# Cross attention: four of seven row units turned in 32x32 blocks on VectorE and through DRAM, instead of on TensorE

## The chip, the cores and the metric

The kernel runs on one core of one Trainium2 chip. The metric is the device time of one execution in microseconds (us). Five engines work side by side: TensorE (PE), VectorE (DVE), ScalarE (ACT), GpSimd (POOL) and SyncE (SP), which here only issues transfers. Sixteen DMA engines move the data.

## The reference

One decoder layer: self attention, cross attention and a mixture of experts, each followed by a residual and a norm. Both kernels differ only in the middle part and in what its memory layout drags along. Cut to that part (32 batches of 56 rows, 1500 context positions, 16 heads of width 128 on 8 key heads):

```
q = (x @ Wq) split in 16 heads          # x: (32, 56, 256)
k, v = ctx @ Wk, ctx @ Wv               # ctx: (32, 1500, 128)
attn = softmax(q @ k.T / sqrt(128) + mask)
x = layernorm(x + (attn @ v) merged @ Wo)
```

The kernel folds Wk into the query side and Wv with Wo into one matrix M per head, so scores are q' @ ctx.T and the output is (attn @ ctx) @ M. Every fp32 product is made of three products of rounded parts, hi*hi + hi*lo + lo*hi.

## The kernel before

It has three phases: phase_a (folded weights, self attention, queries), phase_b (cross attention) and phase_c (routing and experts). Phase_b is about three quarters of the time, and the change is there.

A batch has 16 * 56 = 896 query rows, which are 7 units of 128 rows. A slot is 4 units (even) or 3 units (odd); a pair of batches has 4 slots. Each slot takes CH = 12 steps, so a batch has 24 steps. All engines run the same list of steps in program order, each step with a few pieces of work of different age:

- fill (L817 to L819): three matmuls write 128 rows x 500 scores to one of 3 score banks. VectorE adds the mask, takes the maximum and writes the scores to SBUF (scores, L983), then makes the shift (L991). ScalarE takes the exponential of a unit of 1500 (L901).
- turn (L831): 15 steps later TensorE turns one chunk of 125 positions of every unit of the slot, 128x125 to 125x128, to a turn bank in PSUM. ScalarE rounds it to pT_hi (L895), VectorE makes the rest pT_lo (L997).
- weigh (L850 to L852): two steps later TensorE multiplies the context chunk by pT_hi and pT_lo and sums over the 12 chunks in an output bank.
- the reciprocals of the softmax sums (L1004) are stored to DRAM as single words, 4 bytes each, 512 words for an even slot and 384 for an odd one (store_rden, L908), and fetched again as a row for all partitions (load_rden, L917). VectorE scales the output by them (L1025). After each pair TensorE projects (L860).

SyncE issues the transfers in one order written by hand: q_in, cT_in, mask_in and c_in for each batch (L750 to L766), each after GpSimd has split the one before it in hi and lo (L1099, L1101), and the store of the result (L774). ScalarE's queue issues L908 and L917.

Of the kernel before, what the change touches and what calls it, by code (L numbers as in the profile page):

```python
# [26 lines left out]
ALU = mybir.AluOpType  # L27
# [22 lines left out]
CK = CTX // CH  # L50
FILLS = 3
FW = CTX // FILLS
ROWS = XH * S
UNITS = (4, 3)
SLOTS = 4
WIDE = UNITS[0] * 128
# [11 lines left out]
for width in (NT, EXPERTS * EXPERTS, 128, RP, RP, NT, NT * EXPERTS, 128):  # L68
# [8 lines left out]
Attention = namedtuple("Attention", "sync tensor scalar vector gpsimd edge tail q_split cT_split c_split fill_done fill_taken "  # L77
                       "first_batch_weighed weighed third_slot_turned all_lo projected z_taken y2_stored")
# [45 lines left out]
def phase_a(nc, D, semaphore, M_hi, M_lo, q_in, cT_in, ident, ident_loaded):  # L124
    with ExitStack() as ctx:
# [107 lines left out]
        def sync(sp, load_ahead):  # L233
# [56 lines left out]
            def store_last():  # L290
                store_q(NBLK - 1, range(PARTS))
# [4 lines left out]
            return store_last  # L296
# [331 lines left out]
def phase_b(nc, D, semaphore, edge, opening, M_hi, M_lo, q_in, cT_in, ident, const_loaded):  # L628
    with ExitStack() as ctx:
        def sb(name, shape, dt=F32):  # L630
            edge[name] = nc.sbuf_base
            return ctx.enter_context(nc.sbuf_tensor("b_" + name, shape, dt))

# [9 lines left out]

        oT = sb("oT", [128, XH, 2, S])
        oT_hi = sb("oT_hi", [128, XH, 2, S], F32R)
        oT_lo = sb("oT_lo", [128, XH, 2, S], F32R)
        y1_res = sb("y1_res", [PAIR, F])
# [4 lines left out]
        sb("spare", [128, 2480])  # L652
        pT_hi = sb("pT_hi", [CK, 3, WIDE], F32R)
        pT_lo = sb("pT_lo", [CK, 3, WIDE], F32R)
        p = [None, sb("p1", [128, UNITS[1], CTX])]
        rden_all = sb("rden_all", [128, 2, WIDE])
# [6 lines left out]
        c_in = sb("c_in", [CK, CH * CD])  # L663
        c_hi = sb("c_hi", [CK, 2, CH * CD], F32R)
        c_lo = sb("c_lo", [CK, 2, CH * CD], F32R)
        mask_in = sb("mask_in", [128, CTX], U8)
        mask_add = sb("mask_add", [128, 2, CTX], BF16)
        half = sb("half", [PAIR, 1])
        top = sb("top", [128, 2, UNITS[0], FILLS + 1])
        top_min = sb("top_min", [128, FILLS + 1])  # L670
        shift = sb("shift", [128, 2, UNITS[0]])
        den = sb("den", [128, 2, UNITS[0]])
        rden = sb("rden", [128, 2, UNITS[0]])
        p[0] = sb("p0", [128, UNITS[0], CTX])
        edge["end"] = nc.sbuf_base
# [3 lines left out]
        q_loaded, cT_loaded, c_loaded, mask_loaded = sem("q_loaded"), sem("cT_loaded"), sem("c_loaded"), sem("mask_loaded")  # L679
        res_loaded, y2_stored = sem("res_loaded"), sem("y2_stored")  # L680
        q_split, cT_split, c_split, mask_ready = sem("q_split"), sem("cT_split"), sem("c_split"), sem("mask_ready")
# [3 lines left out]
        rden_done, rden_stored = sem("rden_done"), sem("rden_stored")  # L685
        rden_loaded = [sem("rden_loaded_even"), sem("rden_loaded_odd")]
# [4 lines left out]
        STEPS = SLOTS * CH  # L691
        TURN_LAG = CH + 3
        PV_LAG = TURN_LAG + 2


        RDEN_AT, STORE_AT, LOAD_AT = 3, 4, 11
        SCALE_AT, ROUND_AT = 4, 5
        LATE_SLOTS, LOAD_LATE, SCALE_LATE = range(2), 2, 3
        PROJECT_AT, NORM_AT, NORM_OUT_AT = CH + 10, CH + 11, 2 * CH + 8
        OT_OPS = 2  # L700
        TAIL = PV_LAG + 3
# [7 lines left out]
        def units(slot):  # L709
            return UNITS[slot % 2]  # L710

        unit0 = [sum(units(k) for k in range(slot)) for slot in range(SLOTS + 1)]
        PUNITS = unit0[SLOTS]
        PFILLS = FILLS * PUNITS

        def fills_at(n):

            slot, k = n // CH, n % CH
            count = FILLS * units(slot)
            return [(slot, m) for m in range(count) if m * CH // count == k]  # L720

        def slot_before(i, slot, k):

            return i + (slot - k) // SLOTS, (slot - k) % SLOTS

# [1439 lines left out]
```

## Time and profile before

| | |
|---|---|
| time, median of 3 runs | 1717.78 us (1717.73 to 1717.91) |
| span of the profiled execution | 1718.6 us |
| mean granted TensorE clock | 0.994 |
| TensorE busy | 1685.0 us, 98% |
| VectorE busy | 1221.3 us, 71% |
| ScalarE busy | 937.2 us, 55% |
| GpSimd busy | 664.6 us, 39% |
| moved by DMA | 140.29 MB, mean 82 GB/s |

The profiled execution has no time of its own beside its span; the span is 0.8 us above the median of the runs. A line such as "L983 DVE ... x672 | 451.9, 673 | 58.9" says that line 983 of the kernel ran 672 times on VectorE, was busy for 451.9 us in all, took 673 ns each and that its engine idled 58.9 us just before it.

### The profile page before, as it was taken

Reading aid. Unit: us, or ns where it says so; the run is one execution under the profiler, and the core shown is the slowest. Engines: PE = TensorE matmul, PEld = TensorE weight load, DVE = VectorE, ACT = ScalarE, POOL = GpSimd, SP = SyncE. Lnnn points to the kernel's source line nnn. Section 1 sums busy time; section 2 is a strip of 40 time slices with the busy share of each in tenths; the row PEclk is TensorE's granted clock in tenths of the full one; section 3 lists DMA queues with packets and bytes.
Section 4 is the critical chain, followed back from the end, with each engine's and each line's share of the span. In section 5 each row is a group of like instructions: output and inputs, shape, how many; then the busy total and the mean of one; then the engine's idle time right before and its main releaser. Section 6 shows DMA issues by size and latency. Waiting matters only on the chain.

```text
span 1718.6 us, 28903 instructions
## 1 busy us (share of the span) xinstructions
PE 1685.0 (98%) x10034; PEld 1517.0 (88%) x10034; DVE 1221.3 (71%) x3377; ACT 937.2 (55%) x1717; POOL 664.6 (39%) x417
## 2 busy tenths in 40 slices
PE   7999999999999999999999999999999999999996
PEld 7998889898989898989898989989898989888985
DVE  5655676877787878777778777776878787756557
ACT  5444465656565656565656565565656565644543
POOL 1220344525243333333334343443525341355435
PEclk9999999999999999999999999999999999999998
DMA  5234643423141423333232323232324130431433
GB/s 197 81 132 130 193 95 78 70 68 81 54 97 41 90 44 88 48 86 68 62 68 63 68 63 68 70 66 77 74 61 89 52 57 12 112 114 40 121 90 95
DMA packets 102856, 140.29 MB, mean 82 GB/s; under 512 B 37022, under 2 KB 81728, under 8 KB 102592
## 3 DMA queue, kind: packets, MB, share of 16 engines
q1 hardware_dynamic: 60784, 115.47, 26.8%
q10 hardware_dynamic: 38912, 14.80, 4.0%
q0 software_dynamic: 3024, 8.26, 1.8%
q8 instruction: 79, 1.29, 0.4%
q14 instruction: 57, 0.47, 0.2%
HBM read 113.62 MB, written 24.89 MB: 81 GB/s over the span
## 4 chain that ended last, share of the span: by engine, by line
PE 93%; DVE 2%; issue 1%; ACT 1%; DMA 1%; POOL 0%; another core or an unknown queue 0%; POOLq 0%; SPq 0%; ACTq 0%; DVEq 0%
PE b_turn L831 17%; PE b_out L850 9%; PE b_out L851 9%; PE b_out L852 9%; PE b_score L817 9%; PE b_score L819 9%; PE b_score L818 9%; PE b_out L860 5%; PE a_bank L344 5%; PE c_gate L1513 2%; PE c_down L1540 1%; PE a_bank L370 1%; PE a_bank L395 1%; PE a_bank L424 1%; PE a_bank L417 1%
## 5 line engine op out<-in xcount | busy, mean ns | idle before, releaser
L895 ACT CAST b_pT_hi<-b_turn 125x512 fp32r<-125x512 f32 (+1 forms) x768 | 406.8, 530 | 543.0 <-PE b_turn L831 539.8
L997 DVE TENSOR_TENSOR b_pT_lo<-b_turn,b_pT_hi 125x512 fp32r<-125x512 f32 (+1 forms) x768 | 478.0, 623 | 259.7 <-ACT b_pT_hi L895 254.2
L983 DVE CUSTOM_DVE_ANT_0 b_p<-b_score,b_mask_add 128x500 f32<-128x500 f32 x672 | 451.9, 673 | 58.9 <-PE b_turn L831 24.4
L831 PEld LDWEIGHTS b_turn<-ident,b_p 128*125 128x125 f32 x2688 | 409.4, 186 | 55.2
L831 PE MATMUL b_turn<-ident,b_p 128*125 128x128 f32 x2688 | 418.1, 272 | 0.0
L901 ACT ACTIVATE b_p<-b_p,b_shift 128x1500 f32<-128x1500 f32 x224 | 347.5, 1551 | 2.1 <-DVE b_top_min L991 2.1
L850 PE MATMUL b_out<-b_pT_hi,b_c_hi 125*128 125x512 f32 (+1 forms) x768 | 346.5, 451 | 0.7 <-DVE b_pT_lo L997 0.6
L1135 POOL TENSOR_TENSOR b_oT_lo<-b_oT,b_oT_hi 128x896 fp32r<-128x896 f32 x32 | 67.6, 2112 | 624.5 <-ACT b_oT_hi L925 588.0
L851 PE MATMUL b_out<-b_pT_lo,b_c_hi 125*128 125x512 f32 (+1 forms) x768 | 280.9, 366 | 0.0
L852 PE MATMUL b_out<-b_pT_hi,b_c_lo 125*128 125x512 f32 (+1 forms) x768 | 280.5, 365 | 0.0
L817 PE MATMUL b_score<-b_cT_hi,b_q_hi 128*128 128x500 f32 x672 | 262.9, 391 | 0.0
L819 PE MATMUL b_score<-b_cT_hi,b_q_lo 128*128 128x500 f32 x672 | 260.2, 387 | 0.0
L818 PE MATMUL b_score<-b_cT_lo,b_q_hi 128*128 128x500 f32 x672 | 259.8, 387 | 0.0
L852 PEld LDWEIGHTS b_out<-b_pT_hi,b_c_lo 125*128 125x128 f32 x768 | 144.2, 188 | 17.9
L819 PEld LDWEIGHTS b_score<-b_cT_hi,b_q_lo 128*128 128x128 f32 x672 | 126.1, 188 | 25.8
L850 PEld LDWEIGHTS b_out<-b_pT_hi,b_c_hi 125*128 125x128 f32 x768 | 145.7, 190 | 1.5 <-DVE b_pT_lo L997 1.4
L851 PEld LDWEIGHTS b_out<-b_pT_lo,b_c_hi 125*128 125x128 f32 x768 | 145.9, 190 | 0.0
L818 PEld LDWEIGHTS b_score<-b_cT_lo,b_q_hi 128*128 128x128 f32 x672 | 128.1, 191 | 14.2
L817 PEld LDWEIGHTS b_score<-b_cT_hi,b_q_hi 128*128 128x128 f32 x672 | 126.2, 188 | 14.1
L1101 POOL TENSOR_TENSOR b_c_lo<-b_c_in,b_c_hi 125x1536 fp32r<-125x1536 f32 x32 | 111.9, 3497 | 2.7
L1101 POOL TENSOR_TENSOR b_cT_lo<-cT_in,b_cT_hi 128x1500 fp32r<-128x1500 f32 x31 | 106.3, 3428 | 2.6
L860 PE MATMUL b_out<-M_lo,b_oT_hi 128*112 128x256 f32 x256 | 71.8, 280 | 0.0
(250 smaller groups left out, 2402.1 us busy)
## 6 DMA issues: line engine op xcount, KB each, us to landing
cT_in<-in_ctxT SPq DMA_DIRECT2D x32, 750.0 KB, 9.8
b_c_in<-in_ctx SPq DMA_DIRECT2D x32, 750.0 KB
q_store<-a_fold_in_or_q_stage SPq DMA_DIRECT2D x16, 896.0 KB, 4.2
q_in<-q_store SPq DMA_DIRECT2D x32, 448.0 KB, 7.1
b_rden_all<-rden_store ACTq DMA_DIRECT2D x32, 256.0 KB, 3.6
b_rden_all<-rden_store ACTq DMA_DIRECT2D x32, 192.0 KB, 3.7
b_mask_in<-in_mask SPq DMA_DIRECT2D x32, 187.5 KB, 9.4
slot_store<-c_y2T SPq DMA_DIRECT2D x35, 128.0 KB, 1.7
```

The source lines that it names most:

```text
L817: pe.matmul(out, q_hi[b][:, rows], cT_hi[b][:, keys], start=True, stop=False)
L818: pe.matmul(out, q_hi[b][:, rows], cT_lo[b][:, keys], start=False, stop=False)
L819: pe.matmul(out, q_lo[b][:, rows], cT_hi[b][:, keys], start=False, stop=True).then_inc(fill_done, 1)
L831: mm = pe.transpose(turn_bank[n % 3][0:CK, u * 128:(u + 1) * 128], p[slot % 2][:, u, c * CK:(c + 1) * CK], ident[:])
L850: pe.matmul(out, hi, pT_hi[:, n % 3, 0:w], start=(c == 0), stop=False)
L851: pe.matmul(out, hi, pT_lo[:, n % 3, 0:w], start=False, stop=False)
L852: pe.matmul(out, lo, pT_hi[:, n % 3, 0:w], start=False, stop=(c == CH - 1)).then_inc(pv_done, 1)
L895: act.copy(pT_hi[:, n % 3, 0:w], turn_bank[n % 3][0:CK, 0:w]).then_inc(hi_done, 1)
L901: act.activation(row, row, ACT.Exp, bias=shift[:, slot % 2, u:u + 1], scale=float(X_SCALE), accum_out=den[:, slot % 2, u:u + 1]).then_inc( ...
L983: dve.tensor_tensor_reduce(out=p[slot % 2][:, u, keys], in0=score_bank[j][:, 0:FW], in1=mask_add[:, b, keys], scale=1.0, scalar=-3.0e38, o ...
L997: dve.tensor_tensor(pT_lo[:, n % 3, 0:w], turn_bank[n % 3][0:CK, 0:w], pT_hi[:, n % 3, 0:w].bitcast(F32), ALU.subtract).then_inc(lo_done, 1)
L1101: pool.tensor_tensor(lo, src, hi.bitcast(F32), ALU.subtract).then_inc(done, 1)
```

## The change

The four units of the even half of a batch are no longer turned by TensorE. Their way to the weighing is new:

1. VectorE turns each unit in 32x32 blocks with one instruction over 4 x 12 x 32 = 1536 elements (turn_blocks), at steps 5, 9, 13 and 17 of the batch, into one tile, by_block. It waits until the store of the block before it has landed.
2. SyncE stores by_block to DRAM, 128 partitions of 6144 bytes (store_p), one store for each unit.
3. After the next batch's first such store, SyncE issues 16 fetches (load_keyed): for each unit four, each filling 32 partitions with 4 rows of 1536 bytes. Together they fill keyed, 128 partitions of 16 x 384 words, one buffer.
4. ScalarE rounds each chunk to pT_hi (keyed_round), GpSimd makes the rest in place (keyed_rest) and TensorE weighs it (weigh_even) in steps 16 to 27 after the batch's own 24.

The three odd units still go by TensorE. The loop goes by batches of 24 steps instead of pairs. The roundings of the context parts move from GpSimd to ScalarE (cT_round at step 1, c_round at step 8). The stores of the reciprocals stand at step 16 (even) and at step 2 of the next batch (odd). The context values have two buffers, c_raw, loaded once the batch two before is weighed. The projection is spread over 4 steps. Phase_c gets a new memory layout and a longer tail of steps (24 to 52).

```diff
+            def store_p(m, u):
+                sp.wait_ge(blocks_turned, EVEN * m + u + 1)
+                if m >= 2:
+                    sp.wait_ge(keyed_loaded, 16 * QUADS * EVEN * (m - 1))
+                sp.dma_start(D["p"][m % 2, u].rearrange("q a n -> q (a n)"),
+                             by_block[:].rearrange("q al b j -> q (al b j)")).then_inc(p_stored, 16)
+            def load_keyed(m, u):
+                if m:
+                    sp.wait_ge(pv_done, whole(m - 1))
+                sp.wait_ge(p_stored, 16 * EVEN * (m + 1))
+                for a in range(QUADS):
+                    sp.dma_start(keyed[32 * a:32 * (a + 1), QUADS * u:QUADS * (u + 1), :],
+                                 D["p"][m % 2, u, :, a].rearrange("(b i) n -> i b n", i=32)).then_inc(keyed_loaded, 16)
...
+            for m in range(B):
+                if m >= 2:
+                    load_c(m)
+                if m:
+                    store_p(m, 0)
+                    for u in range(EVEN):
+                        load_keyed(m - 1, u)
+                if m + 2 < B:
+                    load_q(m + 2)
+                if m:
+                    store_p(m, 1)
+                store_p(m, 2)
+                if m + 2 < B:
+                    load_cT(m + 2)
+                    load_mask(m + 2)
+                store_p(m, 3)
...
+            def turn_blocks(m, u):
+                dve.wait_ge(exp_done, PUNITS * m + u + 1)
+                dve.wait_ge(p_stored, 16 * (EVEN * m + u))
+                own = row(m, u)
+                keys = bass.AP(own.tensor, own.offset, [own.ap[0], [32, QUADS], [CK, CH], [1, 32]])
+                dve.transpose(by_block[:], keys).then_inc(blocks_turned, 1)
...
+            def keyed_round(m, c):
+                if c == 0:
+                    act.wait_ge(keyed_loaded, 16 * QUADS * EVEN * (m + 1))
+                act.wait_ge(pv_done, STEPS * m + CH + c - 2)
+                act.copy(by_blocks(pT_hi[:, c % 3, :]), keyed_chunk(keyed, c)).then_inc(hi_done, 1)
...
+            def keyed_rest(m, c):
+                pool.wait_ge(hi_done, STEPS * m + CH + c + 1)
+                pool.tensor_tensor(keyed_chunk(keyed_lo, c), keyed_chunk(keyed, c),
+                                   by_blocks(pT_hi[:, c % 3, :]).bitcast(F32),
+                                   ALU.subtract).then_inc(keyed_lo_done, 1)
```

## Rows read from the trace of the kernel before

**Rows 1.** The page: busy time of the engines.
```profile
PE 1685.0 (98%) x10034; PEld 1517.0 (88%) x10034; DVE 1221.3 (71%) x3377; ACT 937.2 (55%) x1717; POOL 664.6 (39%) x417
```
**Rows 2.** The page: the chain of work that ended last.
```profile
PE 93%; DVE 2%; issue 1%; ACT 1%; DMA 1%; POOL 0%; another core or an unknown queue 0%; POOLq 0%; SPq 0%; ACTq 0%; DVEq 0%
PE b_turn L831 17%; PE b_out L850 9%; PE b_out L851 9%; PE b_out L852 9%; PE b_score L817 9%; PE b_score L819 9%; PE b_score L818 9%; PE b_out L860 5%; PE a_bank L344 5%; PE c_gate L1513 2%; PE c_down L1540 1%; PE a_bank L370 1%; PE a_bank L395 1%; PE a_bank L424 1%; PE a_bank L417 1%
```
**Rows 3.** The timeline, ScalarE's queue: DMA issues of the reciprocals (start, duration).
```profile
709.94 0.33 ACTq L917 DMA_DIRECT2D b_rden_all<-rden_store  x1
718.80 0.38 ACTq L908 DMA_DIRECT2D rden_store<-b_rden  x1
736.88 0.38 ACTq L908 DMA_DIRECT2D rden_store<-b_rden  x1
791.88 0.33 ACTq L917 DMA_DIRECT2D b_rden_all<-rden_store  x1
```
**Rows 4.** The timeline, TensorE in one step with four units.
```profile
739.02 0.39 PE L817 MATMUL b_score<-b_cT_hi,b_q_hi 128*128 128x500 f32 x1
739.71 0.60 PE L831 MATMUL b_turn<-ident,b_p 128*125 128x128 f32 x4
740.07 0.47 PE L850 MATMUL b_out<-b_pT_hi,b_c_hi 125*128 125x512 f32 x1
740.38 0.40 PE L851 MATMUL b_out<-b_pT_lo,b_c_hi 125*128 125x512 f32 x1
740.61 0.40 PE L852 MATMUL b_out<-b_pT_hi,b_c_lo 125*128 125x512 f32 x1
```
**Rows 5.** Groups by line and shape.
```profile
L983 DVE CUSTOM_DVE_ANT_0 b_p<-b_score,b_mask_add 128x500 f32<-128x500 f32 x672 | 451.9, 673 | 58.9 <-PE b_turn L831 24.4 <-PE b_score L819 14.9
L983 DVE DVE_READ_ACCUMULATOR2_ANT b_top<- 128x1 f32 x672 | 55.6, 83 | 0.0
L997 DVE TENSOR_TENSOR b_pT_lo<-b_turn,b_pT_hi 125x512 fp32r<-125x512 f32 x384 | 264.6, 689 | 187.2 <-ACT b_pT_hi L895 183.0 <-issue 0.5
L997 DVE TENSOR_TENSOR b_pT_lo<-b_turn,b_pT_hi 125x384 fp32r<-125x384 f32 x384 | 213.4, 556 | 72.6 <-ACT b_pT_hi L895 71.1 <-issue 0.5
L895 ACT CAST b_pT_hi<-b_turn 125x512 fp32r<-125x512 f32 x384 | 224.1, 584 | 311.1 <-PE b_turn L831 309.3 <-issue 1.8
L1101 POOL TENSOR_TENSOR b_cT_lo<-cT_in,b_cT_hi 128x1500 fp32r<-128x1500 f32 x31 | 106.3, 3428 | 2.6
```
**Rows 6.** Windows: engines' busy time, granted clock, DMA share, GB/s; fastest stretch.
```profile
16.00:20.00 4.00, 4.00 (x32) 3.35 (x31) 2.08 (x4) 1.00 (x4) 0.00 (x0) 1.00 1.06 441
```
**Rows 7.** The timeline, SyncE's queue: a fetch of c_in, and two fetches of cT_in.
```profile
703.53 0.29 SPq L766 DMA_DIRECT2D b_c_in<-in_ctx  x1
721.31 0.33 SPq L756 DMA_DIRECT2D cT_in<-in_ctxT  x1
755.46 0.35 SPq L756 DMA_DIRECT2D cT_in<-in_ctxT  x1
```
**Rows 8.** Windows behind these issues.
```profile
706.00:709.00 3.00, 3.00 (x28) 3.00 (x27) 0.00 (x0) 0.00 (x0) 0.00 (x0) 1.00 0.31 131
722.00:724.00 2.00, 2.00 (x14) 1.89 (x13) 1.80 (x6) 1.96 (x4) 0.67 (x1) 1.00 2.33 48
...
726.00:728.00 2.00, 2.00 (x15) 1.86 (x14) 1.87 (x6) 1.37 (x2) 0.00 (x0) 1.00 0.57 24
...
730.00:732.00 2.00, 2.00 (x13) 1.81 (x12) 1.78 (x8) 0.95 (x3) 0.00 (x0) 1.00 0.97 324
757.00:760.00 3.00, 3.00 (x19) 2.67 (x17) 2.61 (x10) 1.12 (x4) 0.00 (x0) 1.00 0.89 299
```
**Rows 9.** All landings of cT_in, of 750 KB each.
```profile
DMA to landing us min/median/max: 4.3/9.8/11.3
```
**Rows 10.** The page, DMA issues (count, KB each, median us to landing).
```profile
q_store<-a_fold_in_or_q_stage SPq DMA_DIRECT2D x16, 896.0 KB, 4.2
slot_store<-c_y2T SPq DMA_DIRECT2D x35, 128.0 KB, 1.7
```

More of the change, by code:

```diff
@@ new lines, in fills_at, with unit_ends, parity, behind @@
+        def fills_at(n):
+            return [f for f in range(PFILLS) if fill_step(f) == n]
+        def unit_ends(n, late):
+            return [f // FILLS for f in range(FILLS - 1, PFILLS, FILLS) if fill_step(f) + late == n]
+        def parity(u):
+            return (0, u) if u < EVEN else (1, u - EVEN)
+        def behind(m, n, at, count=1):
+            for k in range(3):
+                if at <= n + STEPS * k < at + count and 0 <= m - k:
+                    return m - k, n + STEPS * k - at
+            return None
@@ new lines, in units_behind, with row, whole, keyed_chunk @@
+        def units_behind(m, n, late, last):
+            ends = [] if last else [(m, u) for u in unit_ends(n, late)]
+            return ends + ([(m - 1, u) for u in unit_ends(n + STEPS, late)] if m else [])
+        def row(m, u):
+            return p[0][:, (EVEN * m + u) % EVEN_DEEP, :] if u < EVEN else p[1][:, u - EVEN, :]
+        def whole(m):
+            return STEPS * (m + 1)
+        def keyed_chunk(tensor, c):
+            return tensor[0:CK, :, 32 * c:32 * (c + 1)]
+        def by_blocks(ap):
+            return ap.rearrange("p (g j) -> p g j", j=32)
@@ L797, in sync @@
-            loads(1, first=True)
-            with sp.Fori(2, NPAIR) as i:
-                loads(i)
-            store(NPAIR - 2)
-            residual(NPAIR - 1)
+                load_mask(0)
+                load_c(0)
+            store_last_part, wait_stored = opening.sync(sp, load_ahead)
+            load_q(1)
+            load_cT(1)
+            load_mask(1)
+            load_c(1)
+            for part in range(len(opening.stored)):
+                if part >= 2:
+                    store_p(0, part - 2)
+                store_last_part(part)
@@ L854, in project @@
-            def project(i):
-                pe.wait_ge(oT_lo_done, 2 * (i + 1))
-                for h in range(XH):
+                    if m == 0:
+                        pe.wait_ge(*opening.taken[1])
+                    else:
+                        pe.wait_ge(oT_done, OT_OPS * (2 * m - 1))
+                    pe.wait_ge(c_lo_done, m + 1)
+                pe.wait_ge(lo_done, CH * m + c + 1)
+                out, (hi, lo) = out_bank[1][:, 0:w], values(m, c)
+                pe.matmul(out, hi, pT_hi[:, c % 3, 0:w], start=(c == 0), stop=False)
@@ L861, in project @@
                                        start=(h == 0 and n == 0), stop=(h == XH - 1 and n == len(terms) - 1))
[L862 to L878 removed]
+                if part == parts - 1:
+                    mm.then_inc(proj_done, 1)
@@ L1224, in phase_c @@
         count_r = queries.take("c_count_r", [1, RP])
-        places_2, tiles_2 = odd.again(), odd.again()
+        ones, half = queries.take("c_ones", [128, 128]), queries.take("c_half", [128, 1])
+        turned_p.at = edge["p1"] - 2 * 4 * H_DEEP * 512
         h_hi = turned_p.take("c_h_hi", [128, H_DEEP, 512], F32R)
```

787 lines of the change are left out of this document (403 added, 384 removed).

## The prediction

> **What bounds the kernel now.** I read the page first: TensorE is busy for 98% of the span, VectorE for 71%, ScalarE 55%, GpSimd 39% [rows 1]. The chain of waits says the same of the path: 93% is TensorE, and the turning L831 alone is 17% of it [rows 2]. So matmuls in program order set the time. The fetch of the reciprocals that closes a pair of batches is issued at 709.94 and again at 791.88 [rows 3]: 81.94 us for two, 41.0 us a batch. Whatever is taken from TensorE is gained until something else takes longer than the rest of the batch. Transfers matter nowhere yet. So I next look for what the new transfers would cost.
>
> **What is removed.** One step of an even slot shows four turnings at 739.71 and the weighing behind them at 740.07, 0.36 us. The first weighing matmul takes 0.31 us to the next, the others 0.23 [rows 4], 0.08 more, which I also lay to the turnings. 12 steps x 0.44 = 5.3 us a batch. With nothing else in the way the batch would take 41.0 - 5.3 = 35.7 us.
>
> **What VectorE gets.** It loses 12 rests of 512 columns, 12 x 0.689 = 8.3 us, and gets four block turnings of 1536 elements. No row shows one. The two shapes of L997 differ by 133 ns for 128 columns [rows 5], 1.04 ns an element and 0.16 us fixed: 1.76 us each, 7.0 us in all. Bounds: half the time per element (0.96 us) and twice (3.4 us). With 21 scorings at 0.673 + 0.083, 12 odd rests at 0.556 [rows 5], and some 4 us of small work, VectorE has about 33.6 us in a batch: just below 35.7, no bound yet but no reserve either. After a stall it can't catch up.
>
> **What ScalarE and GpSimd get.** ScalarE rounds as often as before, 0.584 us [rows 5], from SBUF now, and two context parts more (some 3.3 us): it has 45% idle, which hides it. GpSimd gets 12 rests of 512 elements: 3428 ns for 1500 is 2.29 ns each [rows 5], so 1.2 us, 14 us a batch on an engine that had 16 us of work in 41. It fits, 1.2 us against 1.4 us for a TensorE step. Both cost nothing while their inputs are there.
>
> **What the transfers cost: the ring.** The step that I think decides is the order of SyncE's queue. Block turning 2 (step 13) overwrites the one block tile and waits for store 1. Store 1 stands in the queue behind store 0, all 16 fetches and the fetch of q. I follow the ring from the end of block turning 0, taking transfers as served in the order of issue:
> - issue 0.4; store 0, 0.786 MB at the fastest rate that the trace shows, 441 GB/s [rows 6], 1.8
> - the 16 fetches, 3.146 MB: K
> - q, 0.459 MB: 1.0; store 1: 1.8; landing 1.4 (128 KB take 1.7 to land [rows 10], less 0.3 of moving): together 6.4 + K
> - block turning 2, 1.76, and the scoring behind it, 0.76: 2.5. TensorE can be three banks ahead and no more, so it stands at the fill of step 18 until then.
> - TensorE from step 18 to the fill of step 5 of the next batch: 10 fills at 0.69 and 10 weighings of 512 columns at 0.70 [rows 4], an odd weighing of 0.5, three turnings of three units at 0.33, and the last fill 0.7: 16.1
> - VectorE scores, makes a rest and turns block 0: 0.76 + 0.56 + 1.76 = 3.1
>
> The sum is 28.1 + K a batch, if that is more than 35.7.
>
> **K.** No row shows a fetch that fills 32 partitions. Above it stands 441 GB/s, reached with all 128 partitions: 7.1 us. Below stands the only big fetch here that doesn't go over all 128, c_in with 125: issued at 703.53 [rows 7], it runs at 131 GB/s [rows 8]; at that rate K is 24.0 us. The new fetches resemble neither end more; I take the geometric middle, 240 GB/s and K = 13.1 us.
>
> The Trainium skill has a rule that speaks against this edit ("SBUF — State Buffer", the DMA port swizzle): a fetch to partitions 0 to 31 reaches only 8 of 16 ports, some 218 GB/s at best. With it K would be 14.4, the batch 1.3 longer, and the time below 40 us longer. No run so far shows it.
>
> **The fetch of c and the store of single words.** The fetch of c_in (0.768 MB at 131 GB/s, 5.9 us) now stands just before store 0. Counting from the landing of store 1, the weighing that frees its buffer ends at about 16.3 us and block turning 0 at 21.7: alone it adds at most 0.5. But the trace shows a hole. The even reciprocals, 512 words of 4 bytes, are stored at 718.80 [rows 3]; cT_in is issued at 721.31 [rows 7], and the DMA moves 48 and 24 GB/s in the windows at 722 and 726, and 324 only from 730 [rows 8]. The cT_in issued at 755.46 meets no store, and 299 GB/s flow at 757 [rows 7, 8]. Landings of cT_in between 4.3 and 11.3 us say it for all 32 [rows 9]. So behind such a store everything stands for some 11 us. In the new order the odd store (384 words) is issued at about 14.2 us of the same count, right ahead of the c fetch. Behind the odd store of before (736.88, [rows 3]) nothing was issued for ten microseconds, so its hole isn't seen: nothing, or by words three quarters of 11.2, 8.4 us. Then c starts at 22.6 and ends at 28.5, and store 0 is 6.4 us late. Bounds for this term c: 0.5 to 6.4; I take 3. The even store's hole (step 16) falls on cT_in, mask and store 3, which have 11 steps until they are waited for; I cost it at nothing, and if that cover is gone block turning 0 is late next.
>
> The skill's page "DMA: Bandwidth & Descriptors" (Specifications) says that below 512 B the engines read, modify and write. The hole above agrees in kind; by that rule the odd store would have its hole too, c would be 6.4 and the time some 105 us above my forecast.
>
> **Sum.** 28.1 + 13.1 + 3.0 = 44.2 us a batch, 3.2 above 41.0. Over 31 batches +99 us. Once: the last batch's fetches have no fills to hide under. They start at step 27, take K + 2 = 15 us, and some 9 us of odd turning and weighing cover them: +6. The first batch runs at VectorE's pace, some 25 us against about 19 us of matmuls: +6. Against the span, 1718.6 + 111 = 1830; against the median of the runs, 0.8 lower, **1829 us**.
>
> **Rivals.**
> - *The transfers keep up (ends faster).* The fetches run near 441 GB/s and the odd store makes no hole. The ring is 28.1 + 7.1 + 0.5 = 35.7, TensorE's own sum. 1717.8 - 31 x 5.3 + 12 = 1566 us. It decides from K + c below 12.9: with c = 0.5 fetches faster than 254 GB/s. For it: a store of q in small rows, 896 KB, lands in 4.2 us [rows 10]. Against it: c_in's 131 and the hole. All of its cases up to no change together: 24%.
> - *The transfers are worse than I take.* K above 18 or the whole hole: with K = 18 and c = 6.4 the batch takes 52.5, 1717.8 + 31 x 11.5 + 12 = 2086; with K = 24 it is 58.5 and 2272. For it: c_in's row; that even and odd store make two holes in a batch. Against: c_in's row has a shape that no new fetch has. 17%.
> - *VectorE is the bound.* The transfers keep up, but a block turning takes 3.4 us: 33.6 + 6.4 = 40.0 a batch, 1717.8 - 31 x 1.0 + 12 = 1699. For it: no row of that operation. Against: every VectorE row runs near 1 ns an element. 5%.
> - *My forecast*, the ring between 42 and 50 us: 54%.
>
> **Range and chances.** The forecast alone gives 1760 to 2010. The first rival has its bulk at 1566 to 1640, and I can't leave all of it out: 1590 to 2000. A change of 0.2% (3.4 us) is what a measurement can tell here. Faster 27% (the first rival without its last sliver, and most of the third), same 3%, slower 70%.
>
> **What would show it.** In the profile after: the period of a batch from two issues of the same line; TensorE's busy share clearly below 98% with idle time before the fills or the even weighing, released by VectorE's scoring or GpSimd; VectorE's block turning waiting on the DMA of store_p, at the third of the four most; a ScalarE wait at its first keyed round on keyed's DMA. The rate in the windows where only the 16 fetches move gives K at once: 441, 240 or 131 GB/s. A window near 0 GB/s behind the odd store shows c; if bytes flow there, that term falls. If block turning 2 doesn't wait, the ring is wrong, and either TensorE runs at 35.7 us a batch or a cause I haven't named sets it. If the stores pass the fetches in the engines, my assumed order of service falls, and with it most of the loss.

## The result and the profile after

The changed kernel takes **2190.88 us** (median of 4 runs, 2184.44 to 2195.93), the kernel before 1717.76 beside it: ratio 1.2751, 95% interval 1.2723 to 1.2778. It is slower, as forecast, but by 473 us, not by 111, and outside the range. The profiled execution has a span of 2192.8 us and a mean granted clock of 0.894 (0.994 before).

The page of the kernel after (these answer to [rows 1, 2]; then, in 40 equal slices of the span, TensorE's busy tenths, the granted clock in tenths and the DMA share in tenths):

```profile
PE 1684.7 (77%) x8498; PEld 1437.7 (66%) x8498; DVE 1189.4 (54%) x3134; ACT 1018.9 (46%) x1780; POOL 1038.6 (47%) x726
...
PE   8997577676768677868686878676867787849897
...
PEclk9999789898989898888888989898989888979999
DMA  4247577777777777777777777777777777573233
...
DMA 48%; PE 15%; DVE 13%; ACT 5%; issue 4%; POOL 3%; SPq 2%; DVEq 0%; ACTq 0%; POOLq 0%
DMA b_c_raw<-in_ctx 24%; DMA p_store<-b_by_block 23%; DVE b_by_block L1086 7%; ACT b_p L971 2%; PE b_out L912 2%; POOL b_keyed_over L1238 2%; PE b_out L913 2%; PE b_out L914 2%; DVE b_p L1067 2%; SPq L802 2%; PE c_gate L1632 1%; PE b_score L864 1%; PE b_score L866 1%; PE b_score L865 1%; PE b_turn L878 1%
```

No engine is near full. The path is half DMA, and its first name is not the fetches of the weights but the fetch of the context values, c_raw; the stores of the turned blocks come second. The clock is lowest, 7 tenths, in the two slices where TensorE is least busy (5 and 4 tenths).

SyncE's queue over one batch, kernel after (start, us, line, what):

```profile
1007.12 0.29 SPq L786 DMA_DIRECT2D b_c_raw<-in_ctx  x1
1012.46 0.33 SPq L792 DMA_DIRECT2D p_store<-b_by_block  x1
1012.88 15.62 SPq L802 DMA_DIRECT2D b_keyed<-p_store  x16
1028.54 0.63 SPq L772 DMA_DIRECT2D q_in<-q_store  x1
1029.69 14.05 SPq L792 DMA_DIRECT2D p_store<-b_by_block  x2
...
1061.53 0.27 SPq L786 DMA_DIRECT2D b_c_raw<-in_ctx  x1
1066.87 0.35 SPq L792 DMA_DIRECT2D p_store<-b_by_block  x1
```

The same stretch in the chain of waits (start, us, what) and the long waits of the whole span (us in total, times, longest):

```profile
1007.12 18.39 DMA b_c_raw<-in_ctx
1027.89 1.78 DVE b_by_block L1086
1029.69 11.83 DMA p_store<-b_by_block
1041.61 1.79 DVE b_by_block L1086
1043.42 4.09 DMA p_store<-b_by_block
1047.60 1.78 DVE b_by_block L1086
...
1061.53 18.89 DMA b_c_raw<-in_ctx
```
```profile
ACT b_c_hi L1003 <- DMA b_c_raw<-in_ctx: 327.5, 30, 12.5
DVE b_by_block L1086 <- DMA p_store<-b_by_block: 251.0, 62, 13.2
...
ACT b_pT_hi L964 <- DMA b_keyed<-p_store: 88.7, 27, 7.3
```

Read it so: c_raw is issued first and lands 18.4 us later, behind much of what was issued after it. ScalarE, which must round it at step 8, stands 11.4 us and makes no odd chunk; VectorE waits for those chunks before turning 1; so store 1 is issued only at 1029.7, its landing takes 11.8 more, and turning 2 waits for that. Turning 2 is where the prediction looked, but two links that it didn't have come ahead of it. The chain names only the link that ended last, and here another ends almost with it: SyncE itself is not through with the fetches and q before 1029.17 (1028.54 + 0.63), so without the wait for c_raw, and all else as it is, store 1 would be issued only 0.5 us sooner. The period here is 54.4 us (1012.46 to 1066.87).

The words of the odd reciprocals are stored at 1004.71. Windows of the kernel after behind that (busy us and count of each engine, then clock, DMA share, GB/s; answering to [rows 8]):

```profile
1004.00:1007.00 3.00, 3.00 (x18) 2.56 (x17) 2.12 (x8) 1.36 (x4) 0.86 (x1) 1.00 0.07 1
1007.00:1013.00 6.00, 6.00 (x37) 5.58 (x36) 5.87 (x15) 4.91 (x7) 3.19 (x3) 1.00 0.22 24
1013.00:1016.00 3.00, 3.00 (x20) 2.69 (x19) 2.81 (x10) 1.08 (x4) 3.00 (x2) 1.00 0.87 216
1016.00:1020.00 4.00, 4.00 (x32) 3.87 (x32) 0.04 (x2) 0.00 (x0) 3.78 (x2) 1.00 1.04 230
1020.00:1024.00 4.00, 1.25 (x9) 0.94 (x7) 0.00 (x0) 0.00 (x0) 0.00 (x0) 1.00 1.06 193
1024.00:1028.00 4.00, 0.00 (x0) 0.00 (x0) 0.58 (x2) 2.46 (x4) 0.91 (x1) 0.76 1.01 267
1028.00:1032.00 4.00, 3.97 (x16) 3.95 (x17) 3.77 (x7) 1.67 (x3) 2.57 (x1) 0.50 1.09 242
```

The hole is there: for some 8 us behind the store almost nothing moves, and for the last 6 of them c_raw has been issued and gets 24 GB/s. Then c_raw, store 0 and the fetches go together at 190 to 270 GB/s with every engine of the DMA taken (share 1.0). TensorE idles from 1021 to 1028 and works in the 4 us afterwards at a granted clock of 0.50, the 1.2 GHz level.

### The profile page after: what moved, and what is told of

Read it like the earlier page. It is cut to its first block, busy times and chain, and to the rows that moved or that the text cites. A ratio compares the mean times of both kernels' runs of the same rounds, so it can differ in the third digit from the quotient of the medians.

```text
span 2192.8 us, 26254 instructions
## 1 busy us (share of the span) xinstructions
PE 1684.7 (77%) x8498; PEld 1437.7 (66%) x8498; DVE 1189.4 (54%) x3134; ACT 1018.9 (46%) x1780; POOL 1038.6 (47%) x726
## 4 chain that ended last, share of the span: by engine, by line
DMA 48%; PE 15%; DVE 13%; ACT 5%; issue 4%; POOL 3%; SPq 2%; DVEq 0%; ACTq 0%; POOLq 0%
DMA b_c_raw<-in_ctx 24%; DMA p_store<-b_by_block 23%; DVE b_by_block L1086 7%; ACT b_p L971 2%; PE b_out L912 2%; POOL b_keyed_over L1238 2%; PE b_out L913 2%; PE b_out L914 2%; DVE b_p L1067 2%; SPq L802 2%; PE c_gate L1632 1%; PE b_score L864 1%; PE b_score L866 1%; PE b_score L865 1%; PE b_turn L878 1%
## 5 line engine op out<-in xcount | busy, mean ns | idle before, releaser
L1238 POOL TENSOR_TENSOR b_keyed_over<-b_keyed,b_pT_hi 125x512 fp32r<-125x512 f32 x372 | 467.0, 1282 | 445.3 <-ACT b_pT_hi L964 445.3
L1091 DVE TENSOR_TENSOR b_pT_lo<-b_turn,b_pT_hi 125x384 fp32r<-125x384 f32 x384 | 213.0, 556 | 377.6 <-ACT b_pT_hi L957 372.1
L1086 DVE STREAM_TRANSPOSE b_by_block<-b_p 128x1536 f32<-128x1536 f32 x128 | 227.0, 1773 | 252.2 <-DMA p_store<-b_by_block 251.0
L896 PE MATMUL b_out<-b_pT_hi,b_c_hi 125*128 125x384 f32 x384 | 170.4, 444 | 236.0 <-DVE b_pT_lo L1091 236.0
L964 ACT CAST b_pT_hi<-b_keyed 125x512 fp32r<-125x512 f32 x384 | 218.8, 613 | 258.0 <-PE b_out L914 96.6
L912 PE MATMUL b_out<-b_pT_hi,b_c_hi 125*128 125x512 f32 x384 | 180.6, 470 | 186.5 <-POOL b_keyed_over L1238 184.4
L957 ACT CAST b_pT_hi<-b_turn 125x384 fp32r<-125x384 f32 x384 | 179.8, 477 | 263.6 <-PE b_turn L878 257.7
L878 PEld LDWEIGHTS b_turn<-ident,b_p 128*125 128x125 f32 x1152 | 193.9, 195 | 29.5
L1003 ACT CAST b_c_hi<-b_c_raw 125x1536 fp32r<-125x1536 f32 x32 | 47.1, 1471 | 327.5 <-DMA b_c_raw<-in_ctx 327.5
L878 PE MATMUL b_turn<-ident,b_p 128*125 128x128 f32 x1152 | 195.7, 280 | 0.0
L913 PE MATMUL b_out<-b_keyed_over,b_c_hi 125*128 125x512 f32 x384 | 162.7, 424 | 0.0
```

The lines of the kernel that those rows point to most:

```text
L878: mm = pe.transpose(turn_bank[c % 3][0:CK, u * 128:(u + 1) * 128], p[1][:, u, c * CK:(c + 1) * CK], ident[:])
L896: pe.matmul(out, hi, pT_hi[:, c % 3, 0:w], start=(c == 0), stop=False)
L912: pe.matmul(out, hi, own_hi, start=(c == 0), stop=False)
L964: act.copy(by_blocks(pT_hi[:, c % 3, :]), keyed_chunk(keyed, c)).then_inc(hi_done, 1)
L1086: dve.transpose(by_block[:], keys).then_inc(blocks_turned, 1)
L1091: dve.tensor_tensor(pT_lo[:, c % 3, :], turn_bank[c % 3][0:CK, 0:w], pT_hi[:, c % 3, 0:w].bitcast(F32), ALU.subtract).then_inc(lo_done, 1)
```

## The experiments

The theory after the result: a chain through c_raw (hole, landing, ScalarE at step 8, turning 1), then the ring as predicted. The rival: the DMA's time for all bytes (341 MB against 140) sets the time, whatever the order. fetch_128, all_three and cheap_two_first put the weights in wrong places: they show times, not kernels to use. Each run stands with its change against the kernel after or the one named; "before" ran beside each and stayed within 1716.3 to 1719.7 us.

### Three single changes and all of them

```diff
 # rows_stored: VectorE turns rden [128, 2, 32] into rden_rows, four stores of u rows
-                act.dma_start(D["rden"][m, par, 0:128 * u].rearrange("(u q) -> q u", q=128),
-                              rden[:, par, 0:u], allow_slow_non_contiguous=True)
+                for b in range(4):
+                    act.dma_start(D["rden"][m, par, 0:128 * u].rearrange("(u b i) -> b u i", b=4, i=32)[b],
+                                  rden_rows[32 * b:32 * b + u, par, :])
 # c_in_128
-                sp.dma_start(c_raw[m % 2][:], D["ctx"][m])
+                sp.dma_start(c_raw[m % 2][0:rows], D["ctx"].rearrange("b k n -> (b k) n")[CK * m:CK * m + rows])
 # fetch_128
-                    sp.dma_start(keyed[32 * a:32 * (a + 1), QUADS * u:QUADS * (u + 1), :],
-                                 D["p"][m % 2, u, :, a].rearrange("(b i) n -> i b n", i=32))
+                    sp.dma_start(keyed[:, QUADS * u + a, :], D["p"][m % 2, u, :, a])
```

> The reciprocals reach DRAM as runs of 128 bytes (VectorE turns them in 32x32 blocks first, four small stores instead of one) and no longer as 512 and 384 single words. Theory A: the period of 54.9 us a batch is the fetch of c_in (18.4 us from issue to landing, held up by the hole behind the odd word store) followed by the ring block turning 1, store 1 behind the 16 fetches, block turning 2. Without the hole c lands some 7 us earlier: about 48 us a batch, 1950 to 2000 us. Theory B: the plain volume in the DMA engines sets the period, 16 us of slow fetches and as much again of stores and loads; a hole only moves work: within 1% of 2191 us.

Measured: 1997.36 us, ratio 1.1626 (1.1593 to 1.166): 194 us off. It moves the same bytes (341.54 MB), so the rival, bytes whatever the order, is out.

> The fetch of the context values takes 128 rows instead of 125 (three rows of the next batch that nobody reads). Theory A: it then goes over all DMA engines and isn't overtaken by the 16 fetches: it lands soon after the hole, some 8 us earlier, about 47 us a batch, 1930 to 1990 us. Theory B (volume): the bytes are the same, within 1% of 2191 us. Theory C: the hole alone holds c, the spread doesn't matter: within 1% too, and the profile still shows 16 to 18 us from issue to landing.

Measured: 2110.82, ratio 1.2287 (1.2239 to 1.2335): 80 off, less than theory A promised and more than B or C allowed. ScalarE's wait for c_raw falls from 327.5 to 144.1 us, and VectorE's for the stores rises from 251.0 to 385.7.

> Each of the 16 fetches fills 128 partitions with one row of 1536 bytes, instead of 32 partitions with four such rows; bytes, packets and count are the same, but the weights arrive in the wrong places, so the output is not the reference's. Ring (theory A): the fetches' 16 us fall to 7 to 9 us, c is less disturbed and store 1 lands 8 us earlier: 44 to 47 us a batch, 1850 to 1950 us. Theory D, the size of the packets (1536 bytes, read from DRAM) is what makes the fetches slow, not the partitions: no change, within 1% of 2191 us, and the 16 issues still take some 16 us.

Measured: 2058.98, ratio 1.1985 (1.1852 to 1.2118): 132 off, about half of the least that the ring promised; ScalarE's wait for c_raw stays, 308.9 us.

> All three edits together: reciprocals stored as 128-byte runs, c_in over 128 rows, fetches over 128 partitions (weights in the wrong places, so the output is not the reference's). Theory A: the ring is 28 + 8 + 1 = 37 us or TensorE's 36 us a batch: 1580 to 1660 us, below the kernel before. Theory B (volume): 9 MB a batch at some 250 GB/s is 36 us and the stores wait on each other: above 1800 us.

Measured: 1824.42, ratio 1.062 (1.0589 to 1.0651): 366 off, of 406 that the three give singly. That is far above theory A's 1580 to 1660, and the number lies where theory B put it; B is out by rows_stored, and late_two_first below moves 341.5 MB in 1786 us. Windows of this kernel while its fetches move, then its longest DMA wait:

```profile
940.00:944.00 4.00, 4.00 (x30) 3.81 (x29) 1.24 (x3) 1.23 (x3) 3.81 (x2) 1.00 1.07 390
944.00:948.00 4.00, 4.00 (x30) 3.85 (x29) 2.05 (x7) 0.94 (x3) 0.00 (x0) 1.00 1.05 402
```
```profile
DVE b_by_block L1090 <- DMA p_store<-b_by_block: 177.2, 89, 8.2
```

With 128 partitions the fetches move at 390 GB/s in the first window; q and store 1 are issued from 942.69 on and share the second. What is left is the ring of the prediction.

The rows show too how 125 rows of c_raw differ from 128. Each time it moves nearly alone, in rows_two with 125 rows (issued at 1023.71) and in all_three with 128 (issued at 927.54):

```profile
1027.00:1028.00 1.00, 1.00 (x8) 0.92 (x8) 1.00 (x2) 0.19 (x1) 1.00 (x1) 1.00 0.32 135
```
```profile
929.00:930.00 1.00, 1.00 (x8) 0.88 (x7) 0.91 (x4) 1.00 (x2) 0.00 (x0) 1.00 0.93 362
```

The fetch of 125 rows keeps 0.32 of the sixteen DMA engines' time busy, by estimate (0.32 x 16) as much as five of them, and the one of 128 rows 0.93.

### Which word store, and the order alone

```diff
 # rows_odd: as rows_stored, for the odd reciprocals alone
+                if par == 0:
+                    act.dma_start(D["rden"][m, par, 0:128 * u].rearrange("(u q) -> q u", q=128),
+                                  rden[:, par, 0:u], allow_slow_non_contiguous=True)
 # c_late (GpSimd's remainder of c_raw moves behind the keyed ones as well)
                 if m:
                     store_p(m, 1)
+                if m >= 2:
+                    load_c(m)
-        CT_HI_AT, C_HI_AT = 1, 8
+        CT_HI_AT, C_HI_AT = 1, 23
```

> The kernel after with the store of the odd reciprocals alone in rows of 128 bytes; the even ones are still 512 single words. The prediction costed the hole behind the even store at nothing and the one behind the odd store at up to 6.4 us a batch. If that is right, this kernel takes all of the 194 us that both together gave: 1990 to 2030. If each store's hole costs alike, 2080 to 2110. If the even store's is the one that counts, because no step of its surroundings has slack left in this kernel, over 2130.

Measured: 2016.18, ratio 1.172 (1.1691 to 1.1749). The odd store is worth 175 of the 194 us. The prediction had chosen the right one of the two.

> Only order is changed against the kernel after: the fetch of c_raw is issued behind store 1 instead of ahead of store 0, ScalarE rounds it at step 23 instead of step 8, and GpSimd's remainder of it stands behind the twelve keyed remainders. The same bytes move. Theory 1 (the late input holds ScalarE, and with it VectorE's turnings, 11.4 us of a period of some 55 us, and the fetch is ahead of store 0 in the queue): most of that wait goes, 5 to 8 us in each of 14 batches, so 2075 to 2120 us, and the row of ScalarE's wait for the landing of c_raw, 327.5 us now, falls under 60. Theory 2 (the 16 DMA engines' time for all bytes sets the period, whatever the order): within 1% of 2191, and the idle time comes back at other waits, the landings of the stores and of the keyed fetches first.

Measured: 2288.98, ratio 1.332 (1.3269 to 1.337), 98 us slower: both theories missed. The waits of this kernel:

```profile
DVE b_by_block L1086 <- DMA p_store<-b_by_block: 569.8, 90, 14.1
...
ACT b_pT_hi L964 <- DMA b_keyed<-p_store: 194.1, 31, 9.8
```

ScalarE's wait for c_raw is gone, and VectorE's for the stores has more than doubled: c_raw now moves between store 1 and store 2, and with one block tile each store's landing is waited for. This place in the queue, at least, is not free.

### The ring, cut in two ways

The base now has both reciprocals in rows and c_raw of 128 rows.

```diff
 # rows_c_split
                     store_p(m, 0)
-                    for u in range(EVEN):
+                    for u in (0, 1):
                         load_keyed(m - 1, u)
+                    store_p(m, 1)
+                    for u in (2, 3):
+                        load_keyed(m - 1, u)
 # rows_two (c_raw of 125 rows)
-EVEN_DEEP = 3
+EVEN_DEEP = 2
-        by_block = sb("by_block", [128, QUADS, CH, 32])
+        by_block = [sb(f"by_block{b}", [128, QUADS, CH, 32]) for b in range(2)]
-                dve.wait_ge(p_stored, 16 * (EVEN * m + u))
+                dve.wait_ge(p_stored[u % 2], 16 * ((EVEN * m + u) // 2))
```

> The reciprocals stored as rows of 128 bytes and the fetch of c_raw made of 128 rows, together; the fetches of the weights keep their 32 partitions. The two alone saved 194 and 80 us. Theory 1 (each removes its own part of the chain): 1900 to 1935 us. Theory 2 (time for bytes decides): the two parts are different engine time too, so again about 1917; it is the base for the next two kernels, and their differences from it tell the theories apart. If the two removed the same wait, 1960 to 1997.

Measured: 1994.90, ratio 1.1619 (1.1598 to 1.1641). With the words gone the 128 rows of c_raw give nothing clear (2.5 us), though they take ScalarE's wait for c_raw from 39.4 to 2.0 us; 1960 to 1997 was expected for the case that both remove the same wait. In this ring that wait is not what sets the period.

> As the kernel before it in this list (rows of 128 bytes, c_raw of 128 rows), with one change of order in SyncE's queue: of the sixteen fetches eight come ahead of store 1 and eight behind it, and q behind them all. Theory 1 (store 1 stands behind sixteen fetches and q, and turning 2 waits for its landing): the landing of store 1 comes 5 to 8 us sooner in each batch, so 75 to 120 us off, 1800 to 1850. Theory 2 (time for bytes): within 1% of the base. Theory 3 (the second eight fetches now land too late for ScalarE's first rounding of them at step 14): the wait moves there, and the time lies between the base less 40 us and above the base.

Measured: 1973.27, ratio 1.1484 (1.1465 to 1.1503), 22 us off where the ring promised 75 or more. VectorE's wait for the stores fell from 343.6 to 82.5 us; ScalarE's for the fetches rose from 197.1 to 244.3. The number is the one that theory 3 gave.

> All of the order changes on the base: eight fetches, store 1, eight fetches, q, then the fetch of c_raw, which ScalarE rounds at step 23. Theory 1: nothing is left ahead of store 0 or of store 1 but eight fetches, so a further 10 to 60 us off the split one, 1750 to 1830. Theory 2: within 1% of the base. If TensorE's bound of 35.7 us a batch were reached, about 1570 us; that is not expected, since four stores with turnings one behind the other, and the landing of sixteen fetches, remain.

Measured: 2045.19, ratio 1.1902 (1.1883 to 1.1922), 72 us slower than rows_c_split where up to 60 off were expected: slower again, as c_late.

> The kernel with both reciprocals stored in rows (1997 us), and two buffers for the turned blocks with two semaphores for their stores, paid for with one row buffer of p0 less (two instead of three): turning 2 no longer waits for the landing of store 1. The ring as predicted (turning 0, store 0, sixteen fetches, store 1, turning 2) would be cut: if it sets the period, 8 us or more in each batch, 1870 to 1890. The new theory is a second ring: the weights' one fetched buffer is free at step 3, its fetches are issued only behind store 0 of step 5 (5.8 us later), the last lands some 21 us after the first is issued, and twelve steps of keyed weights follow. By it nothing of that is changed here and the time lies at 1960 to 2000, with VectorE's waits for the landings of the stores gone.

Measured: 1930.21, ratio 1.123 (1.1211 to 1.1248), 67 us under rows_stored (which has one row buffer more). The ring of the prediction promised 107 to 127, the second ring at most 37; neither range holds, and each theory may hold part. VectorE's wait for the stores (328.6 us in rows_stored) no longer shows among the long ones, and this stands in the chain of rows_two and again in the next batch, with 12.10:

```profile
1038.02 11.85 DMA b_keyed<-p_store
```

### The fetches ahead of store 0

```diff
 # rows_two_first; the other kernels with two_first in the name have it too
-                    store_p(m, 0)
                     for u in range(EVEN):
                         load_keyed(m - 1, u)
+                    store_p(m, 0)
```

> The kernel with rows and two block buffers (1930 us), with one change of order: the sixteen fetches are issued ahead of store 0. c_raw's fetch of 125 rows stays at the head of the queue, rounded at step 8. By the second ring (the fetched buffer is free at step 3, twelve keyed steps and the landing of sixteen fetches make the period) the fetches start up to 5.8 us sooner a batch, so most of the 131 us: 1800 to 1850. If it was c_raw's move behind store 1 that gave them, 1900 to 1930.

Measured: 2027.79, ratio 1.1787 (1.1758 to 1.1815): 98 us *slower* than rows_two, where 80 to 130 off were expected. Against this, all order changes with c_raw of 128 rows:

> Both reciprocals in rows, c_raw of 128 rows and fetched behind store 1 (rounded at step 23), two block buffers, and the sixteen fetches ahead of store 0 instead of behind it. Everything is computed. By the second ring the fetches start 5.8 us sooner after the buffer is free, so 15 times 5 to 6 us off: 1900 to 1925. If the DMA engines' time for all bytes is the bound, no better than 1975. If the first ring were all, about 1880 as for the kernel with two buffers.

Measured: 1799.30, ratio 1.0465 (1.0445 to 1.0485). All three expectations, 1880 at the lowest, were too high.

The same place in rows_two and then in rows_two_first: SyncE's issues of c_raw and of the fetches, and ScalarE's rounding of c_raw.

```profile
1023.71 0.27 SPq L787 DMA_DIRECT2D b_c_raw<-in_ctx  x1
1029.05 0.34 SPq L793 DMA_DIRECT2D p_store<-b_by_block  x1
1029.51 8.94 SPq L804 DMA_DIRECT2D b_keyed<-p_store  x16
```
```profile
1032.48 1.48 ACT L1006 CAST b_c_hi<-b_c_raw 125x1536 fp32r<-125x1536 f32 x1 [1.79 <-DMA b_c_raw<-in_ctx]
```
```profile
1022.51 0.29 SPq L787 DMA_DIRECT2D b_c_raw<-in_ctx  x1
1022.91 16.60 SPq L804 DMA_DIRECT2D b_keyed<-p_store  x16
```
```profile
1037.78 1.47 ACT L1006 CAST b_c_hi<-b_c_raw 125x1536 fp32r<-125x1536 f32 x1 [8.29 <-DMA b_c_raw<-in_ctx]
```

No word store stands ahead of either. With 5.3 us of empty queue behind it c_raw is rounded 8.8 us after its issue; with the fetches right behind it, 15.3 us, although it was issued first. Over the 30 batches ScalarE's wait for it is 36.3 us in rows_two and 272.0 in rows_two_first. It doesn't go first; what is issued behind it holds it up. Two more runs tell whether its rows or its place do the harm:

> The kernel with rows, two block buffers and the fetches ahead of store 0 (2028 us), with c_raw fetched by 128 rows instead of 125, still at the head of the queue and rounded at step 8. If the slow 125-row fetch is what the sixteen fetches and store 0 stand behind (they took 16.6 us to issue instead of 8.9), 1820 to 1880. If the place is what counts, because ScalarE still waits for it at step 8, 1960 to 2020.

Measured: 1785.06, ratio 1.0391 (1.0373 to 1.0408). Its c_raw of 128 rows lands after 5.3 us (median), with the same fetches right behind it.

> The same kernel with c_raw's 125-row fetch moved behind store 1, rounded at step 23, instead. If the place counts, close to the kernel with both (1799): 1800 to 1850. If the rows count, it holds up stores 2 and 3 there as it held up the fetches before, 1900 to 1990.

Measured: 1786.04, ratio 1.0401 (1.0384 to 1.0419). Either cure takes 242 us, and with both the kernel is 13 us slower than with one (1799.30): needed early and slow is the harm, and one of the two is enough to avoid. Both numbers lie below every range that was expected. Behind store 1 is now a good place, which it was not in c_late; the kernels differ in three things (rows for words, two block tiles, the fetches first), and which of them does it is not shown. In rows_c_two_first the fetches are issued from 1031.63 to 1039.07 and move alone in the first of these windows; store 0 and q are issued in the second, from 1039.17:

```profile
1034.00:1038.00 4.00, 4.00 (x26) 3.77 (x25) 2.83 (x6) 1.64 (x4) 3.68 (x3) 1.00 1.06 222
1038.00:1042.00 4.00, 3.79 (x23) 3.33 (x22) 3.78 (x13) 2.34 (x5) 4.00 (x2) 1.00 1.08 229
```

That is K: 3.146 MB at 222 GB/s are 14.2 us, and 13.7 at 229, at a DMA share above 1.0: the engines are full, and it is not the issuing, 7.4 us, that limits them.

### Do the words still cost, and what is left

```diff
 # cheap_two_first, on rows_c_two_first
-                for a in range(QUADS):
-                    sp.dma_start(keyed[32 * a:32 * (a + 1), QUADS * u:QUADS * (u + 1), :],
-                                 D["p"][m % 2, u, :, a].rearrange("(b i) n -> i b n", i=32))
+                sp.dma_start(keyed[:, QUADS * u:QUADS * (u + 1), :], D["p"][m % 2, u])
 # best_rest_dve (best_rest_half: at[1] >= CH // 2 alone), GpSimd's loop over them cut
-                if last and (at := behind(m, n, HI_AT + CH, CH)) and at[0] == LAST:
+                if at := behind(m, n, HI_AT + CH, CH):
                     keyed_rest(*at)
```

> The best kernel so far (1799 us) with the reciprocals stored as single words again, as in the kernel before. In the kernel after these stores cost 194 us. If their hole is hidden once two block buffers and the early fetches give slack, as it is hidden in the kernel before, 1800 to 1830. If the hole is 5.5 us of DMA time in each batch wherever it falls, since the queue is now busy for two thirds of the time, 1920 to 2000.

Measured: 1826.86, ratio 1.0631 (1.0613 to 1.0648). The words cost 28 us here and 194 in the kernel after. The hole is still there (odd words stored at 1002.02, fetches issued from 1005.46, 25 and 11 GB/s from 1008 to 1012); what differs is how much waits on it.

> As the one before, but each unit's weights are fetched whole by one transfer over 128 partitions (four instead of sixteen, the same bytes), which puts the weights in wrong places and so weighs the wrong values; the reciprocals, c_raw, the two buffers and the order are as there. It shows what the order still holds once no transfer is slow. By the second ring: the fetches land in 12 us or less, which with twelve keyed steps is under TensorE's 35.7 us a batch, so TensorE decides, 1570 to 1680. If the bytes themselves (9.9 MB a batch) decide, 1720 to 1830, as with the three single changes together (1824).

Measured: 1762.09, ratio 1.026 (1.0243 to 1.0277). The number lies in the range that was given to the bytes, 1720 to 1830, and not in TensorE's. But the engines of the DMA are not full; the window from first to last scoring:

```profile
179.30:1501.10 1321.80, 1193.69 (x6144) 1001.02 (x6143) 969.95 (x2618) 823.42 (x1286) 883.32 (x568) 1.00 0.60 219
```

With a DMA share of 0.60 and a clock of 1.00 the batch takes 41.3 us (1321.8 over 32), not 35.7: neither of the two bounds sets it.

> The best kernel so far (1799 us) with all twelve keyed remainders of a batch computed by VectorE (0.69 us each in the last batch) instead of GpSimd (1.29 us each). TensorE waited 227 us in all for GpSimd's. If GpSimd's length is what is left, 100 to 150 us off, 1650 to 1700. If VectorE, 69% busy there and with 8.3 us a batch more nearly as long as a batch of 42 us, becomes the bound, 1790 to 1850. If the DMA engines' time is the bound, no change.

Measured: 1941.36, ratio 1.1305 (1.1271 to 1.1338).

> As the one before, but only the last six of the twelve keyed remainders are VectorE's, so 4.1 us a batch more for it and 7.7 us less for GpSimd. If GpSimd's length is what is left: 40 to 80 us off, 1720 to 1760, and the kernel with all twelve on VectorE faster still. If both engines' places in the chain count, this one is the faster of the two.

Measured: 1900.41, ratio 1.1062 (1.1043 to 1.108). Moving work off GpSimd costs 101 to 142 us, outside all that was expected but for one point: the half move is the better of the two. What can be seen is in the timeline of best_rest_half, VectorE and then GpSimd:

```profile
1034.88 1.29 DVE L1104 TENSOR_TENSOR b_keyed_over<-b_keyed,b_pT_hi 125x512 fp32r<-125x512 f32 x2
...
1038.86 3.51 DVE L1104 TENSOR_TENSOR b_keyed_over<-b_keyed,b_pT_hi 125x512 fp32r<-125x512 f32 x1 [2.01 <-ACT b_pT_hi L968]
```
```profile
1038.39 3.44 POOL L1237 TENSOR_TENSOR b_c_raw_over<-b_c_raw,b_c_hi 125x1536 fp32r<-125x1536 f32 x1 [6.88 <-ACT b_c_hi L1008]
```

VectorE's remainder takes 0.65 us (two in 1.29) and 3.51 us while GpSimd subtracts. The mean of all is 1131 ns here and 916 in best_rest_dve, the median 687 and 686. How much of the loss this makes is not tested.

None of these kernels beats the one before. The best that compute everything are c128_two_first, 1785.06 us, and late_two_first, 1786.04.

## Why the prediction was wrong

First and last scoring stand at 179.8 and 1483.5 in the kernel before and at 181.0 and 1921.9 after, for 32 batches: 40.7 and 54.4 us. The loss is 32 x 13.7 = 438 us and 36 us once; I had 99 and 12. Of the 36, I had 6: in the 58 us behind the last scoring TensorE is busy for 29.8 us, and was for 56.8 in the kernel before.

The ring, measured in six kernels with one block tile (us, medians of 25 or 26 batches, the first three columns from the end of turning 0). The last column runs from the start of turning 2 to the end of the next turning 0:

| | SyncE has issued q | turning 1 ends | turning 2 starts | second half |
|---|---|---|---|---|
| prediction | 16.3 (q moved) | not reckoned | 19.5 | 21.7 |
| after | 15.8 | 16.6 | 29.7 | 25.3 |
| rows_stored | 10.3 | 7.0 | 23.5 | 25.2 |
| c_in_128 | 11.6 | 10.9 | 26.2 | 25.3 |
| fetch_128 | 14.6 | 16.1 | 24.5 | 25.3 |
| rows_c | 10.3 | 6.2 | 23.1 | 25.3 |
| all_three | 9.8 | 6.1 | 17.5 | 25.3 |

The batch of 44.2 us was 19.5 + 21.7 + 3.0 for c. It came to 55.0 in the median (54.4 over all 32): **three terms of the sum failed**, c (6.2 for 3.0), the first half without it (23.5 for 19.5) and the second half (25.3 for 21.7).

**What is removed.** The 5.3 us of turnings are gone from TensorE. It got nothing for them, since it was no longer the bound.

**VectorE, block turnings.** Estimated 1.76 us, measured 1.773. Right. The rival that VectorE is the bound is out.

**c.** The term failed, in size and place. I put it at 0.5 to 6.4 us of a late store 0. Store 0 wasn't late: it followed the issue of c_raw by 5.3 us with rows as with words (1023.71 to 1029.05, 1007.12 to 1012.46). The hole behind the odd store was real (24 GB/s for 6 us) and the even one was nearly free, as I said: 175 and 19 us. Without the words the first half is 6.2 us shorter, which is all of the 194 us (6.1 a batch) and close to my upper bound; the price is paid as a later landing of store 1.

**ScalarE and GpSimd "cost nothing while their inputs are there".** GpSimd's keyed rest took 1.28 us against 1.2. But the input of ScalarE's new rounding at step 8 wasn't there: 327.5 us of waiting. The sentence had its condition, and I didn't examine it. An instruction moved into an in-order engine brings its wait with it, and every odd chunk and so turning 1 stood behind it. What this link costs by itself is less than its total: in the kernel after turning 1 ends 0.8 us behind SyncE's issue of q, and from rows_stored to rows_c the rest of the wait (39.4 to 2.0 us) goes for a gain of 2.5 us. In rows_two_first, where the wait is 272.0 us, either cure takes 242 us off.

**The ring, first half.** Its last wait, turning 2 on store 1, is right, and all_three shows it bare. But "taking transfers as served in the order of issue" fell. In rows_stored SyncE is through with the queue 6 us sooner than I reckoned (10.3 for 16.3), and store 1 then takes 13.2 us to land where I had 3.2: it is held up by all that is still moving. c_raw too is held up by what is issued behind it, 15.3 against 8.8 us.

**The ring, second half.** I had turning 2, one scoring and then TensorE, all at once released. In these kernels turning 3 starts only some 6.0 us after turning 2, for it waits for store 2 to land (4.09 at 1043.42); then scoring, ScalarE's exponential and rounding and GpSimd's rest follow before TensorE can weigh on, and this stands in the chain:

```profile
1053.02 1.28 POOL b_keyed_over L1238
...
1054.34 0.50 PE b_out L912
```

That is 12.7 us after turning 2 began. The wait for store 2 and this way round over three engines were not in the sum; how the 3.6 us divide between them is not shown. The clock is not the cause. Two second halves of the kernel after, the columns as above:

```profile
987.20:1012.46 25.26, 23.93 (x105) 19.32 (x105) 18.39 (x52) 16.45 (x25) 15.53 (x13) 0.91 0.59 106
1041.61:1066.87 25.26, 21.91 (x104) 17.26 (x103) 18.99 (x53) 16.34 (x25) 16.04 (x14) 1.00 0.60 116
```

At a clock of 0.91 TensorE is busy 2.0 us longer than at 1.00, and the stretch is as long.

**A second ring**, which I hadn't seen, lies close behind: one keyed buffer, free at step 3, filled again only behind store 0. The waits point to it (ScalarE's for the fetches, 244.3 us in rows_c_split, and the 11.85 us in the chain of rows_two), and it may be why a split queue gave 22 us alone and two block tiles 67; no run separates it.

**K.** 13.1 taken; 13.7 to 14.2 measured. Right, about 1 us off. The Trainium skill's rule on 8 of 16 ports ("SBUF — State Buffer", the DMA port swizzle) gave 14.4, from 218 GB/s at best. The trace agrees within 5%: 222 to 229 GB/s for 32 partitions, against 390 for 128.

**The rivals.** "The transfers are worse than I take" is what came, at 2191 within its 2086 to 2272, but this is half luck. Its condition of the whole hole came true, its K above 18 did not. With K = 14 and c = 6.4 my own sum gives 48.5 us a batch and 1962 us; the rest is the first half's order of service and the second half's waits, which no rival had. At 17% it was rated too low: the hole seen in the trace of before [rows 8] was good evidence, and the geometric middle of a term isn't the middle of a sum of waits that feed each other.

**Still open.** Why 41.3 us remain when no transfer is slow. TensorE is 90% busy there; its matmuls wait 63.6 us in all for GpSimd's rests and its weight loads 97.9, in part the same time; the two runs that shorten GpSimd's share lengthen other waits. No more was tried.

## What to carry to other kernels

When work is moved onto an engine that has time to spare, ask for each moved instruction which input it waits for and what stands behind it in that engine's order; the busy share says nothing about that. A wait that is large in the list need not cost what it says: another link may end just ahead of it, as SyncE's queue does here, and only a run that takes it away tells. A transfer with a low rate of its own (131 GB/s, [rows 8]) lands late although it is issued first, if others follow at once: give it all partitions or a late reader. Cures of one chain don't add up: c_raw's 128 rows gave 80 us, nothing clear, or 242 us, and its later place cost 98 us in one kernel and gave 242 in another.

## What was not expected of the hardware

- A store of 384 single words, issued from another queue, held up nearly all transfers of the core for some 8 us: c_raw, issued 2.4 us behind it, moved at 24 GB/s for 6 us. In rows_two, with rows for words, c_raw is at 135 GB/s in the window from 3.3 us behind its issue.
- A fetch of 125 rows moved at 135 GB/s with a DMA share of 0.32, the same bytes in 128 rows at 362 with 0.93.
- The granted clock was 0.50, the 1.2 GHz level, in the 4 us behind an idle stretch of 7 us. The 8498 matmuls are busy 1684.7 us at a mean clock of 0.894 and 1583.3 us in cheap_two_first at 0.988; these 101 us are busy time; of the two second halves shown above, the one with more of it is no longer than the other.
- A VectorE subtraction of 125 x 512 from and to SBUF took 3.51 us instead of 0.65 while GpSimd ran one of 125 x 1536 (3.44 us). Why is not tested; the subtractions with one input in PSUM (L1096) keep their mean of 554 ns in best_rest_dve, as 556 in [rows 5].
